# Second attention: score products over all 128 rows, keys in zero-padded tiles, a ring of two head groups

## The chip, the cores and the metric

The kernel runs on one core of one Trainium2 chip. The metric is the device time of one execution in microseconds (us); the kernel before takes 2373.17 us, the median of three runs.

## The reference

A batch of 8 sequences of 512 tokens and 128 features passes six blocks, each added to its input: `ffn0` (32 experts, 8 chosen), `attn0` (causal softmax attention), `ffn0` again, `ffn1` (8 experts, 2 chosen), `attn1` and `ffn1` again. The change lies in `attn1`, the second attention:

```python
qkv = (x @ w_qkv).reshape(Bx, Sx, H, 3 * HD)          # H = 16 heads, HD = 8
scores = jnp.einsum('bhqd,bhkd->bhqk', q, k) / jnp.sqrt(HD)
w = jax.nn.relu(scores)
attn = w / (jnp.sum(w, axis=-1, keepdims=True) + 1e-6)
out = jnp.einsum('bhqk,bhkd->bhqd', attn, v)
y = x + out @ w_out + b_out
return layernorm(y) * gamma + beta                     # and x = x + this
```

So each head has only 8 numbers per token to sum over in a score.

## The kernel before

The six stages run one after another, each over 8 chunks; a chunk (c0 to c7 here) is one sequence of 512 tokens. All data between stages stays in the on-chip memory `x`. In each stage every engine goes through the same list of slots, and the tables `TAIL`, `PREP`, `QKV_AT` and `PUT_AT` say at which slot an engine does a step of the chunk before (its end, "tail") or of the chunk after (its beginning, "prep"). The engines agree through semaphores only; each executes its own list in order.

Precision: a float32 product is made of three fp32r products (high by high, high by low, low by high), called `products` (lines 375 to 377). For the scores the three are put in one contraction instead: each head has 3 x 8 = 24 rows of parts of q and k, padded to 32 rows. q and k go for that through DRAM: ScalarE and VectorE leave the parts in `attn_parts`, SyncE's queue writes them to `parts_dram` (6 transfers, L1314), and reads them back by groups of four heads, 32 rows per head, so that a group fills 128 partitions.

A chunk of `attn1` has 16 slots: 4 groups of four heads by 4 blocks of 128 keys. In slot n (`pe_attn1`, L752 on) TensorE makes four score products (L767), one per head, each 24 rows deep with 128 key columns as weights and 512 queries streaming. Head j lies in partitions 32j to 32j+24 of `k_st` and `q_st`, so that the four use four different row strips of the array. Then come the products with the values of the slot before (`pv1`, L578): for each of four heads 128 rows and 32 output columns, in two instructions, four column strips side by side. ReLU and the move out of PSUM are done by ScalarE (L880, heads 0, 1 and in six slots 3) and VectorE (L1167, the others). There are four score banks, one for each head, so a head's next score product waits until its bank has been emptied.

Around them, in the same slots: the layernorm of the next chunk (VectorE L890 to L907, TensorE turn L489), its q, k and v (TensorE in slots 4, 5 and 7), the last slot's value product and the output projection of the chunk before (slots 0 and 6), the division by the sums (`take_half`, VectorE L1086 to L1098, once in slot 9 and once in the next chunk's slot 1), and the second layernorm (`y_norm` in slot 7, `y_scale` in slot 9, `y_add` on GpSimd in slot 10).

SyncE's list for a chunk of `attn1` (`dma_body`): wait for the parts of the next chunk, write them, then read the four groups of the next chunk, each as one transfer for q (L1328) and one for k (L1333), each as soon as this chunk has made its last score product with that group. `attn0` already keeps its keys in another form, `k_one`: a tile of 128 partitions for every head, with the head's 32 rows in place and zeros elsewhere; its score products (L687, L709) run over all 128 rows.

Of the kernel before, what the change touches and what calls it, by code (L numbers as in the profile page):

```python
# [16 lines left out]
P = 128  # L17
# [40 lines left out]
QUAD = 4  # L58
NQ = H // QUAD
NBLK = S // 32  # L60
ONE = 1
# [94 lines left out]
class AttnMemory:  # L156


    def __init__(self, which, alloc, part):
        def sb(name, shape, dt, stack=part):  # L160
            return alloc(name, shape, dt, stack)

        self.q_st = sb(which + "_q_st", [P, NQ, S], F32R)
        if which == "attn0":
            self.k_one = sb("k_one", [P, NQ, QUAD, S], F32R)
        else:
            self.k_st = sb(which + "_k_st", [P, NQ, S], F32R)
        self.parts = sb(which + "_parts", [P, 2, 2, S], F32R)
        self.v_tok = sb(which + "_v_tok", [P, NT, NQ, QUAD, HD], F32)
        self.v_st = sb(which + "_v_st", [P, NT, NQ, QUAD, PC], F32)  # L170
        self.attn = sb(which + "_attn", [P, NBLK, PC], F32)
        with ExitStack() as shared:
            stack = shared if which == "attn0" else part
            self.o_turn = sb(which + "_o_turn", [P, NBLK, PC], F32, stack)
            self.aT = sb(which + "_aT", [P, S], F32, stack)
        self.aT_hi, self.aT_lo = sb(which + "_aT_hi", [P, S], F32R), sb(which + "_aT_lo", [P, S], F32R)
        if which == "attn0":
            self.rmax = sb("rmax", [P, 2, NT, QUAD], F32)
        else:
            self.xk = sb("attn1_xk", [P, 2, NT, D], F32)  # L180

# [6 lines left out]
def build(nc, x_in, w0, w1, wa, biases, bd3, rows, consts, out, scratch, mixed):  # L188
    nc.disable_value_cache = True
    ctx = ExitStack()  # L190
    with ctx:
# [12 lines left out]
        ident = ident_r[:, :].bitcast(F32)  # L204
        cbf = sb("cbf", [P, NCONST], BF16)
        bd_parts = sb("bd_parts", [96, NPART, D], BF16)
# [238 lines left out]
        def stacks_in(ch):  # L445

            return 32 * (ch.ga + 1) + 48 * (ch.g + 1 if ch.causal else NB)

# [187 lines left out]
        def weight(eng, ch, p):  # L636

            if p == 0:
                eng.wait_ge(wT_ready, ch.gf + 1)

            if p == 1 and ch.first and ch.s:
                eng.wait_ge(o_turned, 2 * ch.stages_before("attn") * NB)
            eng.wait_ge(hid_ready, ROUND + ch.g * NPS + (p - 1 if p > 1 else p - 2))
            eng.matmul(weight_bank(p)[:, :], cbf[0:NPART * E0, C_SEL0 + p * P:C_SEL0 + (p + 1) * P], wT[:, ch.parity, :],
                       start=True, stop=True).then_inc(wb_ready, 1)

        def pe_ffn1(eng, ch, j):
# [15 lines left out]
            if j % HC == 1:  # L663
                e = j // HC
                if e == 0:
                    eng.wait_ge(wT_ready, ch.gf + 1)
                eng.wait_ge(rb_ready, ROUND + ch.g * E1 + e)
                eng.matmul(bank[4][:, :], cbf[0:NPART * E1, C_SEL1 + e * P:C_SEL1 + (e + 1) * P],  # L668
                           wT[0:NPART * E1, ch.parity, :], start=True, stop=True).then_inc(rb_ps, 1)
# [87 lines left out]
        def pe_attn1(eng, ch, n):  # L757

            quad, kb, i = n // NT, n % NT, ch.g * NS1 + n
            if kb == 0:  # L760
                eng.wait_ge(st_in[quad], stacks_in(ch))
            if n == 0 and ch.first:
                eng.wait_ge(ze_ready, ROUND + ch.stages_before("ffn1") * NB * E1)
            for j in HEAD_ORDER:
                rows_ = slice(PC * j, PC * j + NROW * HD)
                eng.wait_ge(p1_ready[j], ROUND + i)
                eng.matmul(bank[j][:, :], mem1.k_st[rows_, quad, kb * P:(kb + 1) * P], mem1.q_st[rows_, quad, :],  # L767
                           start=True, stop=True).then_inc(s1_ps, 1)
            if n:
                pv1(eng, ch, n - 1)  # L770
# [398 lines left out]
        def dve_tail(eng, step, ch):  # L1169
# [20 lines left out]
            if step == "y_norm":  # L1190
# [3 lines left out]
                eng.wait_ge(kept, ch.g + 1)  # L1194
                xk = mem1.xk[:, ch.parity, :, :]
                v = st.mark(eng.tensor_tensor(xk, ob, xk, ALU.add))
# [9 lines left out]
            if step == "y_scale":  # L1206
                xk = mem1.xk[:, ch.parity, :, :]
                eng.wait_ge(y_rstd_ready, ch.g + 1)
# [6 lines left out]
        def pool_prep(eng, step, ch):  # L1215
# [3 lines left out]
            if step == "keep":  # L1219
                eng.wait_ge(ln_steps.sem, ch.G * 13 + 13)  # L1220
                if not ch.first:
                    eng.wait_ge(x_done, ONE + ch.G - 1)
                eng.tensor_tensor(mem1.xk[:, ch.parity, :, :], xn[:, :, :], row_of(1), ALU.add).then_inc(kept, 1)
            if step == "put":
                for quad in range(NQ):
                    put_values(eng, ch, quad)
        def pool_tail(eng, step, ch):
# [3 lines left out]
            if step == "y_add":  # L1231
                eng.wait_ge(tail.sem, 13 * ch.g + 13)
                xk = mem1.xk[:, ch.parity, :, :]
                eng.tensor_tensor(xk, xk, row_of(2), ALU.mult).then_inc(y_scaled, 1)
# [70 lines left out]
        def write_stacks(eng, ch):  # L1305

            if not ch.first or not ch.causal:
                eng.wait_ge(st_in[NQ - 1], stacks_in(ch) - (80 if ch.causal else 32))
            for i in range(2):
# [7 lines left out]
        def read_stacks(eng, ch, g):  # L1317
# [3 lines left out]
            if not ch.first and ch.causal:  # L1321
                eng.wait_ge(st_ready, (ch.g - 1) * NS0 + (g + 1) * NF)
            elif not ch.first:
                eng.wait_ge(s1_ps, ((ch.g - 1) * NS1 + (g + 1) * NT) * QUAD)
            if ch.causal and ch.first and g == 0:
                eng.wait_ge(k_zeroed, H)
            q_src, k_src = (stacks[i, g * QUAD:(g + 1) * QUAD, :, :] for i in range(2))
            eng.dma_start(ch.mem.q_st[:, g, :].bitcast(F32), q_src.rearrange("h r s -> (h r) s")).then_inc(st_in[g], 16)  # L1328
            if ch.causal:
                for j in range(QUAD):  # L1330
                    eng.dma_start(mem0.k_one[PC * j:PC * (j + 1), g, j, :].bitcast(F32), k_src[j]).then_inc(st_in[g], 16)
            else:
                eng.dma_start(mem1.k_st[:, g, :].bitcast(F32), k_src.rearrange("h r s -> (h r) s")).then_inc(st_in[g], 16)  # L1333

# [17 lines left out]
        def dma_body(eng, s, c):  # L1352
# [10 lines left out]
            if ch.kind == "attn0":  # L1363
# [9 lines left out]
                if not ch.last:  # L1373
                    for g in range(2, NQ):
                        read_stacks(eng, after, g)
            elif after is not None and after.kind[:4] == "attn":
                write_stacks(eng, after)
                for g in range(NQ):
                    read_stacks(eng, after, g)
# [45 lines left out]
        def _(eng):  # L1425
# [24 lines left out]
        def _(eng):  # L1450
# [61 lines left out]
        def _(eng):  # L1512
            for counts in (xnT_ps,):
                eng.sem_inc(counts, ONE)
            for counts in (h_used, h1_used, pv1_done):
                eng.sem_inc(counts, ROUND)
            eng.wait_ge(const_ready, 2 + E1 + 1)
            eng.wait_ge(w_lo_done, len(loads))
# [68 lines left out]
```

## Time and profile before

| | |
|---|---|
| time, median of 3 runs | 2373.17 us (2372.46 to 2374.28) |
| the profiled execution | 2367.19 us, of which the span from first to last instruction is 2365.5 us |
| TensorE busy | 2205.1 us, 93% of the span |
| VectorE, ScalarE, GpSimd busy | 1737.0, 1290.2, 922.0 us |
| mean granted TensorE clock | 0.974 of full speed |
| the second attention | 1612 to 1936 us of the span |

The profile is of one execution. A TensorE instruction's duration contains the pipeline behind it, and instructions overlap; the distance from the start of one to the start of the next says what it costs the engine. "Idle before" with a releaser names who ended the wait.

### The profile page before, as it was taken

To read this page: it belongs to the slowest core of one execution; us is meant where nothing else is said; L and a number is where in the kernel's file an instruction comes from. 1 tells how busy PE (TensorE), PEld (TensorE's weight loads), DVE (VectorE), ACT (ScalarE), POOL (GpSimd) and SP (SyncE) were. 2 spreads that over 40 slices of the span, in tenths; PEclk is the share of its full clock that TensorE was granted. 3 is DMA by queue.
4 is the path that set the end of the run, shared out by engine and by line. 5 is a ranking of instruction groups with operands and counts; after the bars stand their busy time and mean duration, and the time that the engine had idled before them with its cause. 6 is when DMAs were issued, how large, how long until landed. Compare 5 with 4: busy or idle time off the path is not lost.

```text
span 2365.5 us, 45578 instructions
## 1 busy us (share of the span) xinstructions
PE 2205.1 (93%) x11232; PEld 1475.3 (62%) x11232; DVE 1737.0 (73%) x3590; ACT 1290.2 (55%) x2000; POOL 922.0 (39%) x903
## 2 busy tenths in 40 slices
PE   2999999999999889999999999999999999999999
PEld 2666666666666666666777777773323236777776
DVE  4676666777777566667568888876767787888886
ACT  3655565455555656565455555555555554555554
POOL 1555455223332445555434444442121224444443
PEclk9999999999999999999999999998979899999999
DMA  3000002233322000000000000012323200000000
GB/s 147 1 0 0 0 0 63 63 86 104 87 80 80 14 13 14 9 9 16 10 1 1 0 0 0 0 37 89 107 71 98 89 10 5 5 4 4 4 4 10
DMA packets 59566, 78.94 MB, mean 33 GB/s; under 512 B 22784, under 2 KB 27104, under 8 KB 59232
## 3 DMA queue, kind: packets, MB, share of 16 engines
q1 hardware_dynamic: 59488, 77.99, 11.0%
q8 instruction: 38, 0.62, 0.1%
q14 instruction: 40, 0.33, 0.0%
HBM read 48.08 MB, written 29.88 MB: 33 GB/s over the span
## 4 chain that ended last, share of the span: by engine, by line
PE 57%; issue 16%; POOL 11%; DVE 11%; ACT 2%; DVEq 1%; DMA 1%; POOLq 1%; SPq 0%; ACTq 0%
PE pair L375 12%; PE pair L377 10%; PE pair L376 10%; POOL h_lo L1293 10%; PE pair L767 3%; PE bank L578 3%; PE pair L578 3%; PE pair L687 2%; PE pair L709 2%; PE bank L564 2%; PE pair L668 2%; PE bank L375 1%; DVE rmax L1123 1%; PE bank L377 1%; PE bank L376 1%
## 5 line engine op out<-in xcount | busy, mean ns | idle before, releaser
L1299 POOL TENSOR_TENSOR h_lo<-hid,h_hi 128x512 fp32r<-128x512 f32 x256 | 330.4, 1291 | 515.7 <-ACT h_hi L851 515.7
L1293 POOL TENSOR_TENSOR h_lo<-hid,h_hi 128x512 fp32r<-128x512 f32 x272 | 351.5, 1293 | 365.2 <-ACT h_hi L817 364.2
L375 PE MATMUL pair<-xnT_hi,w_hi 128*128 (+1 forms) x1056 | 481.7, 456 | 11.0 <-DVE h_lo L1068 8.9
L377 PE MATMUL pair<-xnT_hi,w_lo 128*128 (+1 forms) x1056 | 419.4, 397 | 0.0
L376 PE MATMUL pair<-xnT_lo,w_hi 128*128 (+1 forms) x1056 | 416.5, 394 | 0.0
L375 PE MATMUL pair<-h_hi,w_hi 128*128 128x512 f32 x784 | 327.8, 418 | 14.7 <-POOL h_lo L1293 12.3
L846 ACT ACTIVATE hid<-pair,bias 128x512 f32<-128x512 f32 x256 | 176.3, 689 | 258.9 <-PE pair L377 256.9
L376 PE MATMUL pair<-h_lo,w_hi 128*128 128x512 f32 x784 | 309.6, 395 | 0.0
L377 PE MATMUL pair<-h_hi,w_lo 128*128 128x512 f32 x784 | 309.1, 394 | 0.0
L1066 DVE TENSOR_SCALAR h_hi<-pair,nb 128x512 fp32r<-128x512 f32 x256 | 191.3, 747 | 117.9 <-PE pair L377 116.7
L817 ACT ACTIVATE h_hi<-hid 128x512 fp32r<-128x512 f32 x272 | 171.6, 631 | 179.3 <-DVE hid L1051 164.7
L375 PEld LDWEIGHTS pair<-xnT_hi,w_hi 128*128 128x128 f32 x1056 | 203.1, 192 | 54.6 <-issue 18.6
L821 ACT ACTIVATE gate<-pair,bias 128x512 f32<-128x512 f32 x272 | 185.7, 683 | 89.4 <-PE pair L377 85.8
L869 ACT ACTIVATE probs<-pair 128x1024 f32<-128x1024 f32 x160 | 163.4, 1025 | 129.3 <-PE pair L709 126.1
L1042 DVE SCALAR_TENSOR_TENSOR prod<-pair,bias,gate 128x512 f32<-128x512 f32 x256 | 191.1, 746 | 55.4 <-ACT gate L821 35.6
L880 ACT ACTIVATE probs<-pair 128x512 f32<-128x512 f32 x304 | 163.3, 598 | 120.0 <-PE pair L767 113.3
L377 PEld LDWEIGHTS pair<-xnT_hi,w_lo 128*128 128x128 f32 x1056 | 199.2, 189 | 45.1
L376 PEld LDWEIGHTS pair<-xnT_lo,w_hi 128*128 128x128 f32 x1056 | 200.8, 190 | 34.3
L375 PEld LDWEIGHTS pair<-h_hi,w_hi 128*128 128x128 f32 x784 | 147.5, 188 | 83.2 <-issue 38.5
L1068 DVE SCALAR_TENSOR_TENSOR h_lo<-pair,nb,h_hi 128x512 fp32r<-128x512 f32 x256 | 192.3, 751 | 9.0
L1278 POOL TENSOR_SCALAR_AFFINE_SELECT probs<-probs 128x512 f32<-128x512 f32 (+1 forms) x160 | 87.0, 543 | 264.7 <-ACT probs L869 264.7
L851 ACT ACTIVATE h_hi<-hid 128x512 fp32r<-128x512 f32 x256 | 161.8, 632 | 28.4 <-PE pair L377 3.7
(183 smaller groups left out, 3648.9 us busy)
## 6 DMA issues: line engine op xcount, KB each, us to landing
parts_dram<-attn_parts SPq DMA_DIRECT2D x96, 256.0 KB, 2.9
attn_q_st<-parts_dram SPq DMA_DIRECT2D x64, 256.0 KB, 2.7
k_one<-parts_dram SPq DMA_DIRECT2D x128, 64.0 KB, 2.4
attn_k_st<-parts_dram SPq DMA_DIRECT2D x32, 256.0 KB, 3.0
stage_w<-in_w_dram SPq DMA_DIRECT2D x32, 130.0 KB, 2.1
stage_w<-in_w_dram SPq DMA_DIRECT2D x6, 512.0 KB, 12.4
x<-in_x_dram SPq DMA_DIRECT2D x1, 2048.0 KB, 7.7
mixed_dram<-attn_aT SPq DMA_DIRECT2D x32, 64.0 KB
```

The costliest lines, as they stand in the source:

```text
L375: eng.matmul(o, w_hi_, v_hi, start=start, stop=False, **kw)
L376: eng.matmul(o, w_hi_, v_lo, start=False, stop=False, **kw)
L377: return eng.matmul(o, w_lo_, v_hi, start=False, stop=stop, **kw)
L817: eng.activation(h_hi[:, q % NH0, :], hid[:, q % NHID, :], ACT.Copy).then_inc(hi_ready, 1)
L821: eng.activation(gate[:, p % 2, :], bank[p % 2][:, :], ACT.Silu, bias=bias[:, BG + p:BG + p + 1]).then_inc(silu_ready, 1)
L846: eng.activation(hid[:, i % NHID, :], bank[j % 3][:, :], ACT.Relu, bias=bias[:, B1 + j:B1 + j + 1]).then_inc(hid1_ready, 1)
L869: eng.activation(probs0[:, fill, :, :], pair[ring(("k", n))][:, :, :], ACT.Exp).then_inc(p0_full, 1)
L1042: eng.scalar_tensor_tensor(dst, bank[2 + p % 2][:, :], bias[:, BU + p:BU + p + 1], gate[:, p % 2, :], ALU.add, ALU.mult).then_inc(prod_rea ...
L1066: eng.tensor_scalar(h_hi[:, j % NH1, :], bank[j % 3][:, :], floor, None, ALU.max).then_inc(hi1v_ready, 1)
L1068: eng.scalar_tensor_tensor(h_lo[:, j % NH1, :], bank[j % 3][:, :], floor, h_hi[:, j % NH1, :].bitcast(F32), ALU.max, ALU.subtract).then_in ...
L1293: eng.tensor_tensor(h_lo[:, p % NH0, :], hid[:, p % NHID, :], h_hi[:, p % NH0, :].bitcast(F32), ALU.subtract).then_inc(lo_ready, 1)
L1299: eng.tensor_tensor(h_lo[:, j % NH1, :], hid[:, j // 2 % NHID, :], h_hi[:, j % NH1, :].bitcast(F32), ALU.subtract).then_inc(lo1p_ready, 1)
```

## The change

`attn1` keeps its keys as `attn0` does, in a `k_one` of its own, but for two groups at a time: group g uses place g modulo 2 (`KRING = 2`). A score product takes all 128 rows of `k_one` and of `q_st`; the zeros take the other heads' rows out of the sum. A group of k now comes in four transfers of 32 rows, one for each head. Since the ring holds two groups, groups 2 and 3 of a chunk are read within the chunk, after slots 3 and 7 have made their score products; SyncE does this ahead of the writes for the next chunk and the reads of its groups 0 and 1. The ring's zeros are set once by VectorE after the first chunk of the first `ffn1`. To find room, the residual tile `attn1_xk` and the selector matrices `sel1` take memory of their own, partly that of `sel0`, which is no longer needed then, and the constants come in three copies instead of one.

```diff
@@ class AttnMemory
-            self.k_st = sb(which + "_k_st", [P, NQ, S], F32R)
+            self.k_one = sb("attn1_k_one", [P, KRING, QUAD, S], F32R)
@@ build: memory
-        cbf = sb("cbf", [P, NCONST], BF16)
+        cbf = sb("cbf", [P, C_SEL0], BF16)
+        with ExitStack() as part:
+            sel0 = sb("sel0", [P, NP * P], BF16, part)
+        attn1_xk = sb("attn1_xk", [P, 2, NT, D], F32)
+        sel1 = sb("sel1", [P, E1 * P], BF16)
@@ pe_attn1
             for j in HEAD_ORDER:
-                rows_ = slice(PC * j, PC * j + NROW * HD)
                 eng.wait_ge(p1_ready[j], ROUND + i)
-                eng.matmul(bank[j][:, :], mem1.k_st[rows_, quad, kb * P:(kb + 1) * P], mem1.q_st[rows_, quad, :],
+                eng.matmul(bank[j][:, :], mem1.k_one[:, quad % KRING, j, kb * P:(kb + 1) * P], mem1.q_st[:, quad, :],
                            start=True, stop=True).then_inc(s1_ps, 1)
@@ write_stacks
-                eng.wait_ge(st_in[NQ - 1], stacks_in(ch) - (80 if ch.causal else 32))
+                eng.wait_ge(st_in[NQ - 1], stacks_in(ch) - 80)
@@ read_stacks
-            elif not ch.first:
-                eng.wait_ge(s1_ps, ((ch.g - 1) * NS1 + (g + 1) * NT) * QUAD)
+            elif not ch.first or not ch.causal and g >= KRING:
+                eng.wait_ge(s1_ps, (ch.g * NS1 + (g - KRING + 1) * NT) * QUAD)
...
-                eng.dma_start(mem1.k_st[:, g, :].bitcast(F32), k_src.rearrange("h r s -> (h r) s")).then_inc(st_in[g], 16)
+            for j in range(QUAD):
+                eng.dma_start(ch.mem.k_one[PC * j:PC * (j + 1), g if ch.causal else g % KRING, j, :].bitcast(F32),
+                              k_src[j]).then_inc(st_in[g], 16)
@@ dma_body
-            elif after is not None and after.kind[:4] == "attn":
+            if ch.kind == "attn1":
+                for g in range(KRING, NQ):
+                    read_stacks(eng, ch, g)
+            if ch.kind != "attn0" and after is not None and after.kind[:4] == "attn":
                 write_stacks(eng, after)
-                for g in range(NQ):
+                for g in range(NQ if after.causal else KRING):
                     read_stacks(eng, after, g)
@@ scalar, start of the program
-            eng.activation(cbf[:, :], stage_c[:, 0:NCONST], ACT.Copy).then_inc(const_ready, 1)
+            for dst, a, b in ((cbf, 0, C_SEL0), (sel0, C_SEL0, C_SEL1), (sel1, C_SEL1, NCONST)):
+                eng.activation(dst[:, :], stage_c[:, a:b], ACT.Copy).then_inc(const_ready, 1)
@@ vector, after the first chunk of the first ffn1
                     eng.wait_ge(x_done, ONE + s * NB)
+                    for i in range(KRING):
+                        eng.memset(mem1.k_one[:, i, :, :].bitcast(F32), 0.0).then_inc(k_zeroed, 1)
```

## Rows read from the trace of the kernel before

**Rows 1.** The page: busy time, share and instructions, by engine.
```profile
PE 2205.1 (93%) x11232; PEld 1475.3 (62%) x11232; DVE 1737.0 (73%) x3590; ACT 1290.2 (55%) x2000; POOL 922.0 (39%) x903
```
**Rows 2.** Windows: stage, length, busy by engine, clock, DMA: first and second attention.
```profile
612.00:960.00 348.00, 323.23 (x2001) 225.46 (x2000) 245.17 (x482) 198.03 (x271) 141.16 (x173) 0.99 0.17 45
1612.00:1936.00 324.00, 296.67 (x1786) 105.27 (x1787) 237.07 (x535) 182.52 (x344) 59.99 (x72) 0.86 0.25 80
```
**Rows 3.** The line of the score products (L767): durations, count, first and last start.
```profile
L767 PE MATMUL pair<-attn_q_st,attn_k_st x512: 477/497/792, 1612.9 to 1934.6; 24*128 24x512 f32 x171
```
**Rows 4.** Timeline of TensorE, slots 6 and 7 of c2: start, duration, instruction.
```profile
1707.29 0.51 PE L767 MATMUL pair<-attn_q_st,attn_k_st 24*128 24x512 f32 x4
1707.73 1.07 PE L578 MATMUL pair<-probs,attn_v_st 128*32 128x512 f32 x8
1708.72 0.33 PE L375 MATMUL bank<-wa_hi,xnT_hi 128*128 128x128 f32 x1
...
1710.21 0.50 PE L767 MATMUL pair<-attn_q_st,attn_k_st 24*128 24x512 f32 x4
```
**Rows 5.** Timeline of TensorE, the q product between column strips and row strips.
```profile
1700.86 0.50 PE L375 MATMUL bank<-xnT_hi,wa_hi 128*128 128x512 f32 x1
1701.20 0.39 PE L376 MATMUL bank<-xnT_lo,wa_hi 128*128 128x512 f32 x1
...
1701.76 0.79 PE L767 MATMUL pair<-attn_q_st,attn_k_st 24*128 24x512 f32 x4
```
**Rows 6.** Timeline of TensorE in the first attention, 128-row scores and column strips.
```profile
700.41 0.71 PE L709 MATMUL pair<-attn_q_st,k_one 128*128 128x512 f32 x2
701.06 0.64 PE L564 MATMUL bank<-probs,attn_v_st 128*32 128x256 f32 x8
```
**Rows 7.** Timeline of TensorE, two slots at the lower clock.
```profile
1681.25 0.80 PE L767 MATMUL pair<-attn_q_st,attn_k_st 24*128 24x512 f32 x4
...
1683.84 0.80 PE L767 MATMUL pair<-attn_q_st,attn_k_st 24*128 24x512 f32 x4
```
**Rows 8.** Windows around two falls of the clock; columns as in rows 2.
```profile
1674.80:1678.20 3.40, 0.81 (x7) 0.31 (x3) 3.24 (x5) 0.81 (x2) 2.89 (x3) 1.00 0.01 2
...
1691.80:1695.20 3.40, 2.73 (x19) 1.26 (x16) 3.12 (x11) 2.56 (x5) 1.28 (x2) 1.00 0.30 108
1695.20:1698.60 3.40, 3.40 (x18) 0.49 (x12) 3.13 (x8) 1.50 (x4) 0.00 (x0) 0.51 0.00 0
```
**Rows 9.** Timeline, slots 9 and 10 of c1: VectorE, then TensorE.
```profile
1673.64 0.72 DVE L1086 STREAM_TRANSPOSE attn_o_turn<-pair 128x512 f32<-128x512 f32 x1
...
1675.92 1.50 DVE L1098 TENSOR_TENSOR attn_attn<-attn_o_turn,rden 128x256 f32<-128x256 f32 x1
1677.34 1.27 DVE L1167 TENSOR_SCALAR probs<-pair 128x512 f32<-128x512 f32 x2
...
1673.39 0.50 PE L767 MATMUL pair<-attn_q_st,attn_k_st 24*128 24x512 f32 x4
...
1678.07 1.38 PE L767 MATMUL pair<-attn_q_st,attn_k_st 24*128 24x512 f32 x3 [2.58 <-DVE probs L1167]
```
**Rows 10.** Timeline of VectorE, slot 1 of c1, the other half of the division.
```profile
1654.99 0.43 DVE L1098 TENSOR_TENSOR attn_attn<-attn_o_turn,rden 128x256 f32<-128x256 f32 x1
```
**Rows 11.** Timeline of SyncE's queue, second and first attention; then a time to landing.
```profile
1702.48 4.43 SPq L1314 DMA_DIRECT2D parts_dram<-attn_parts  x6
1709.74 0.33 SPq L1328 DMA_DIRECT2D attn_q_st<-parts_dram  x1
...
674.48 1.82 SPq L1331 DMA_DIRECT2D k_one<-parts_dram  x4
...
k_one<-parts_dram SPq DMA_DIRECT2D x128, 64.0 KB, 2.4
```
**Rows 12.** Timeline in the first `ffn1`: VectorE's zeroing of the values, TensorE behind it.
```profile
1243.05 1.76 DVE L1481 MEMSET attn_v_st<- 128x2048 f32 x1 [0.38 <-issue]
1246.90 0.49 PE L375 MATMUL pair<-xnT_hi,w_hi 128*128 x1 [0.41 <-DVE h_lo L1068]
```

More of the change, by code:

```diff
@@ L59 @@
 NQ = H // QUAD
+KRING = 2
 NBLK = S // 32
@@ L178, in __init__ @@
             self.rmax = sb("rmax", [P, 2, NT, QUAD], F32)
-        else:
-            self.xk = sb("attn1_xk", [P, 2, NT, D], F32)
 def act_heads(n):
@@ L445, in stacks_in @@
         def stacks_in(ch):
-            return 32 * (ch.ga + 1) + 48 * (ch.g + 1 if ch.causal else NB)
+            return 80 * (ch.ga + 1)
         def filled(ch, use):
@@ L643, in weight @@
             eng.wait_ge(hid_ready, ROUND + ch.g * NPS + (p - 1 if p > 1 else p - 2))
-            eng.matmul(weight_bank(p)[:, :], cbf[0:NPART * E0, C_SEL0 + p * P:C_SEL0 + (p + 1) * P], wT[:, ch.parity, :],
+            eng.matmul(weight_bank(p)[:, :], sel0[0:NPART * E0, p * P:(p + 1) * P], wT[:, ch.parity, :],
                        start=True, stop=True).then_inc(wb_ready, 1)
@@ L667, in pe_ffn1 @@
                 eng.wait_ge(rb_ready, ROUND + ch.g * E1 + e)
-                eng.matmul(bank[4][:, :], cbf[0:NPART * E1, C_SEL1 + e * P:C_SEL1 + (e + 1) * P],
+                eng.matmul(bank[4][:, :], sel1[0:NPART * E1, e * P:(e + 1) * P],
                            wT[0:NPART * E1, ch.parity, :], start=True, stop=True).then_inc(rb_ps, 1)
@@ L1194, in dve_tail @@
                 eng.wait_ge(kept, ch.g + 1)
-                xk = mem1.xk[:, ch.parity, :, :]
+                xk = attn1_xk[:, ch.parity, :, :]
                 v = st.mark(eng.tensor_tensor(xk, ob, xk, ALU.add))
@@ L1206, in dve_tail @@
             if step == "y_scale":
-                xk = mem1.xk[:, ch.parity, :, :]
+                xk = attn1_xk[:, ch.parity, :, :]
                 eng.wait_ge(y_rstd_ready, ch.g + 1)
@@ L1222, in pool_prep @@
                     eng.wait_ge(x_done, ONE + ch.G - 1)
-                eng.tensor_tensor(mem1.xk[:, ch.parity, :, :], xn[:, :, :], row_of(1), ALU.add).then_inc(kept, 1)
+                eng.tensor_tensor(attn1_xk[:, ch.parity, :, :], xn[:, :, :], row_of(1), ALU.add).then_inc(kept, 1)
             if step == "put":
@@ L1232, in pool_tail @@
                 eng.wait_ge(tail.sem, 13 * ch.g + 13)
-                xk = mem1.xk[:, ch.parity, :, :]
+                xk = attn1_xk[:, ch.parity, :, :]
                 eng.tensor_tensor(xk, xk, row_of(2), ALU.mult).then_inc(y_scaled, 1)
@@ L1322, in read_stacks @@
                 eng.wait_ge(st_ready, (ch.g - 1) * NS0 + (g + 1) * NF)
-            elif not ch.first:
-                eng.wait_ge(s1_ps, ((ch.g - 1) * NS1 + (g + 1) * NT) * QUAD)
-            if ch.causal and ch.first and g == 0:
-                eng.wait_ge(k_zeroed, H)
+            elif not ch.first or not ch.causal and g >= KRING:
+                eng.wait_ge(s1_ps, (ch.g * NS1 + (g - KRING + 1) * NT) * QUAD)
+            if ch.first and g == 0:
+                eng.wait_ge(k_zeroed, H + (0 if ch.causal else KRING))
             q_src, k_src = (stacks[i, g * QUAD:(g + 1) * QUAD, :, :] for i in range(2))
             eng.dma_start(ch.mem.q_st[:, g, :].bitcast(F32), q_src.rearrange("h r s -> (h r) s")).then_inc(st_in[g], 16)
[L1329 to L1332, printed above, removed]
-                eng.dma_start(mem1.k_st[:, g, :].bitcast(F32), k_src.rearrange("h r s -> (h r) s")).then_inc(st_in[g], 16)
+            for j in range(QUAD):
+                eng.dma_start(ch.mem.k_one[PC * j:PC * (j + 1), g if ch.causal else g % KRING, j, :].bitcast(F32),
+                              k_src[j]).then_inc(st_in[g], 16)
         def heads_out(eng, ch):
@@ L1516, in _ @@
                 eng.sem_inc(counts, ROUND)
-            eng.wait_ge(const_ready, 2 + E1 + 1)
+            eng.wait_ge(const_ready, 4 + E1 + 1)
             eng.wait_ge(w_lo_done, len(loads))
```

## The prediction

> **What bounds the kernel now.** I read the page first. TensorE is busy for 93% of the span [rows 1], so what counts is how long it takes over its own list and what it waits for. The windows by stage come next, since the change touches one stage: the second attention lasts 324 us, with 128 slots (8 chunks of 16), so 2.53 us a slot, and its granted clock is 0.86 where the first attention has 0.99 [rows 2]. The clock has two levels, 1.2 and 2.4 GHz, so 0.86 means that 28% of the stage, 91 us, ran at the lower one. All 512 score products lie in this stage [rows 3].
>
> The timeline gives the cost of a slot where TensorE waits for nothing. At the upper clock the four score products start together and the value products start 0.44 us later (1707.29 to 1707.73); these take 0.99 us (to 1708.72) [rows 4]. A slot is thus 1.43 us. At the lower clock it is 2.59 us (1681.25 to 1683.84) [rows 7]. The q product costs 0.90 us (1700.86 to 1701.76) [rows 5], as does k; v costs 1.49 us (1708.72 to 1710.21) [rows 4], and I take the same for the projection, which has as many instructions, and 0.6 us for the turn of the normed input. That is about 5.4 us for a full chunk and 43 us for eight.
>
> So the 324 us are made up of 128 x 1.43 = 183, plus 43 for the other products, plus 45 for the lower clock (half of the 91 us), and the 53 that are left are waits of TensorE, 6.6 us a chunk. The largest wait is in slot 10. VectorE spends 3.70 us on the division (1673.64 to 1677.34) before it empties the banks of slot 9, and TensorE stands for 2.6 to 2.9 us [rows 9]. In the window with this wait TensorE was busy for 0.81 of 3.40 us. The clock fell at its end. But it fell too at 1695.2 us, where TensorE had been busy for 2.73 of 3.40 us, with row-strip scores of 24 rows and few value products [rows 8]. Slots with half-filled scores keep the clock up badly; this is what the change can win on.
>
> **Score products over 128 rows: dearer.** They no longer start together: one follows the other. The q product shows what fp32r products of 128 rows and 512 columns cost between column strips and strips: 0.34 us from the first to the second, then 0.56 us for the last two, that is 0.23 and 0.33, since the last one before strips is slower again [rows 5]. The first attention has this very sequence, 128-row scores and then column strips: two products take 0.65 us (700.41 to 701.06) [rows 6], the same 0.32 each at the ends. Four are 0.34 + 0.23 + 0.23 + 0.33 = 1.13 us; I take 1.12. Against 0.44 that is 0.68 more a slot, 87 us for 128 slots. From below, four at the inner pitch of 0.23 give 0.92 us, 61 us in all; from above, twice the 0.65 us of two gives 1.30 us, 110 us. I take 87, because the row it rests on has the same neighbours. Slot floor: 1.12 + 0.99 = 2.11 us.
>
> The Trainium skill has a rule against this change: in "TensorE: Matmul & The Clock Gate", Part 3 (Measured speedup), four row strips with 512 columns gain 3.07 times over doing them one by one. By it the scores would go from 0.44 to 1.35 us, 116 us in all (an estimate from that page); the rows say 2.5 times, and the sum goes by the rows.
>
> **The clock: given back, mostly.** In a slot of 2.11 us TensorE now streams over full rows nearly all the time, so the falls with no long wait (1695.2) go; so do second and third stretches at the lower clock after a fall, since even there it works densely. The first attention, with the same forms, has 0.99 [rows 2]. All 45 us would go. But the wait in slot 10 stays: VectorE's 3.70 us stand. VectorE can begin about 0.5 us after slot 9's first score product, ends 3.7 us later, the first freed bank lets TensorE go on 0.73 us after that (1677.34 to 1678.07) [rows 9]: 4.97 us. TensorE gets there after 1.12 + 0.99 + 0.34 = 2.45 us, and waits 2.5 us, then 0.3 us for the other bank. A wait of this length brought the clock down each time before; with dense work before and behind it I let it fall in two chunks of three, for a stretch of about 3.4 us like 1695.2 to 1698.6 [rows 8], costing half less the wait within it: 1.3 us x 5.4 falls = 7 us. From below 0 (never), from above two stretches in each of 8 chunks, 27 us.
>
> **Waits that the longer slot hides.** VectorE empties two banks in 1.27 us [rows 9], well inside a slot of 2.11, and ScalarE has the other half; so ordinary slots no longer wait. In slots 0 to 3 VectorE has the layernorm, the other half of the division and the turn's input to do, and following it by the durations I get 0.9 us of waiting a chunk. With 2.8 in slot 10 that is 3.7 a chunk, 30 us in all for 53 before: 23 us gained. What is late next in the other slots is TensorE itself.
>
> **SyncE's queue.** A group's k is four transfers, 1.82 us of issue for 0.43 before; per chunk 20 reads for 8. The writes for the next chunk used to start at slot 4 or 5 and are now behind the read of group 3, which waits for slot 7's scores, and behind its landing. Chain from there: q 0.34 and k 1.82 issued, 2.4 to land, six writes 4.43, 2.8 until they have landed (1706.91 to 1709.74), the next group 0's issue 2.2 and landing 2.4: 16.4 us [rows 11]. From slot 7's last score product to the next chunk's slot 0 there are about eight slots, 8 x 2.11 plus the wait of 2.8 plus the last value product 0.99, less the product itself, some 20 us or more. It fits, with 4 us to spare. Groups 2 and 3 have four slots, over 8 us, for 4.6. Cost 0; nothing else waits on SyncE in this stage. At the start three copies of constants in place of one add only fixed parts (the columns are the same), ahead of weights that ScalarE then waits for from DMA: 0, at most 0.5.
>
> **Zeros for the ring.** VectorE's zeroing of 2048 columns takes 1.76 us, and already that one leaves TensorE waiting 0.41 us [rows 12]. Two more are 3.5 us ahead of work TensorE needs: nearly all becomes a wait, and such a wait can bring the clock down once more. I take 4 us; 0 at least if there is slack that I don't see, 7 at most (two stretches at the lower clock).
>
> **Sum.** +87 - 45 + 7 - 23 + 4 = +30 us. The profiled execution's own time is 2367.19 us (span 2365.5), which becomes 2397; it is 6 us below the median of the runs, so the forecast on the median is 2373 + 30 = 2403 us. A difference of about 0.2% (5 us) can be told from none.
>
> **Rivals.**
> A, faster: the change of strips costs nothing any more. If a score slot of 128 rows needs neither the extra 0.1 us at its two ends nor the 0.12 us between value products and scores, scores are 4 x 0.22 = 0.87 and a slot 1.74 us: 128 x 0.31 = 40 us more in place of 87, so 2403 - 47 = 2356 us. It decides from a slot floor of about 1.8 us downwards. For it: row strips are gone. Against it: the value products keep their column strips, and the first attention pays at this very seam [rows 6]. The Trainium skill agrees with the rows here ("TensorEngine Tiling (Array Packing)", Key Properties: changing the tiling mode drains TensorE), and by it A is not to be had. 15%.
> B, nearly even: the wait in slot 10 goes. Its division step took 1.50 us there and 0.43 us in slot 1 [rows 9, 10], while GpSimd's `y_add` ran beside it. Were the two to part in the new order, the division is 2 us shorter, the wait 0.8, and the clock doesn't fall: -16 and -7, 2380 us, and with scores between the forecast and their lower bound (1.02 us, -13) 2367. Against it: `y_add` still follows `y_scale` directly. 12%.
> C, slower still: the transfers come late. If the chain of 16.4 us is 7 us longer, through transfers that crowd each other, slot 0 of seven chunks waits 3 us: +21, 2424 us. For it: there are more and smaller transfers, and the writes stand behind two reads. Against it: the DMA share of the stage is 0.25 [rows 2]. 7%.
> That the change doesn't do what it says I exclude; the same tile form runs in the first attention.
>
> **How the numbers follow.** The forecast has 66%, with its own range of 2377 (scores at 0.92 us) to 2423 (falls at their upper bound). A 15%, B 12%, C 7%. For 8 in 10 I go down into A: 2360 to 2426. Faster (under 2368): A and a part of B, 0.18. Within 0.2% (2368 to 2378): the rest of B and the forecast's lower edge, 0.12. Slower: 0.70.
>
> **What would show it.** In the timeline of the new kernel: four score products about 1.1 us before the value products, and 2.1 us from slot to slot (0.9 and 1.75 would be A). In the windows: the stage 350 us long, its clock at 0.95 or more, with falls only behind slot 10. VectorE's division still 3.7 us and TensorE's wait after it 2.5 (B: 1.7 and none). In SyncE's queue: the read of group 0 landed before slot 0 (C: TensorE released by a transfer). In the first `ffn1`: a wait of TensorE of 3 to 4 us behind the zeroing. The prediction is wrong if the slot floor is not near 2.1 us, or if TensorE's waits shrink by much more than 23 us.

## The result: slower by 0.65%, half of what was forecast

| | time, median | |
|---|---|---|
| before | 2372.82 us | 4 runs, 2368.23 to 2374.28 |
| after | 2387.45 us | 4 runs, 2386.36 to 2388.45 |
| ratio after to before | 1.0065 | 95% interval 1.0047 to 1.0082 |

The forecast was 2403 us, with 2360 to 2426 as its range. The change costs 14.6 us on the medians and 21.3 us between the two profiled executions, since that of before (2367.19 us) was quicker than all four of its runs and that of after (2388.45 us) the longest of its four.

The page of the kernel after, its first line, then the windows of the second attention and of the first (columns as in [rows 2]), then the line of the score products:

```profile
PE 2231.0 (93%) x11232; PEld 1518.5 (64%) x11232; DVE 1741.5 (73%) x3592; ACT 1290.1 (54%) x2002; POOL 922.5 (39%) x903
```
```profile
1622.00:1956.00 334.00, 315.41 (x1779) 143.04 (x1781) 237.34 (x534) 182.10 (x344) 60.26 (x72) 0.98 0.26 81
612.00:960.00 348.00, 323.32 (x1987) 225.54 (x1988) 243.28 (x480) 196.17 (x268) 139.48 (x172) 0.98 0.16 45
```
```profile
L769 PE MATMUL pair<-attn_q_st,attn_k_one x512: 387/397/796, 1621.9 to 1955.2; 128*128 128x512 f32 x171
```

The stage is 11.5 us longer (worked out below) in spite of a granted clock of 0.98 for 0.86 [rows 2]. A single score product has become shorter by its record (397 ns for 497 [rows 3]) and all four together much longer; only the distance from start to start says so. The timeline of TensorE in slots 6 to 8 of c2, which answers to [rows 4]:

```profile
1720.93 1.14 PE L769 MATMUL pair<-attn_q_st,attn_k_one 128*128 128x512 f32 x4
1722.00 1.07 PE L581 MATMUL pair<-probs,attn_v_st 128*32 128x512 f32 x8
1723.00 0.33 PE L378 MATMUL bank<-wa_hi,xnT_hi 128*128 128x128 f32 x1
...
1724.39 1.15 PE L769 MATMUL pair<-attn_q_st,attn_k_one 128*128 128x512 f32 x4
1725.47 1.06 PE L581 MATMUL pair<-probs,attn_v_st 128*32 128x512 f32 x8
1726.46 1.19 PE L769 MATMUL pair<-attn_q_st,attn_k_one 128*128 128x512 f32 x4
1727.59 1.06 PE L581 MATMUL pair<-probs,attn_v_st 128*32 128x512 f32 x8
1728.58 1.19 PE L769 MATMUL pair<-attn_q_st,attn_k_one 128*128 128x512 f32 x4
```

From score to score: 1726.46 to 1728.58 is 2.12 us, of which the scores take 1.13 (1726.46 to 1727.59). The forecast had 1.12 and 2.11. After another 128-row product the scores cost only 1.07 to 1.08 us (1720.93 to 1722.00, 1724.39 to 1725.47), and v costs 1.39 us (1723.00 to 1724.39) for 1.49 before: the seam between products of 128 rows and row strips is gone there.

Where the 21.3 us between the profiled executions lie, by comparing when the same TensorE instruction starts in both: 0.5 us at the start of the first attention, 3.4 us between 740 and 860 us of the span, 5.3 us near 1250 us, 11.5 us in the second attention (1612.91 to 1935.07 before, 1621.93 to 1955.55 after), 0.7 us behind it. The 3.4 us are a clock that fell three times there in this execution and not in that of before, in code that the change doesn't touch. The profiled executions of other kernels below have one such fall there (e2), two (e6) or none (e1); how often each kernel has them is not known.

The lengths of the slots, from the starts of their first score product (my table; a star: started at the lower clock):

| slot | 0 | 1 | 2 | 3 | 4 | 5 | 6 | 7 | 8 | 9 | 10 | 11 | 12 | 13 | 14 | 15 | chunk |
|---|---|---|---|---|---|---|---|---|---|---|---|---|---|---|---|---|---|
| before, c1 | 1.18 | 2.61 | 2.69 | 2.46 | 2.53 | 2.92 | 2.92 | 1.43 | 2.17 | 1.59 | 6.26 | 2.59* | 1.91* | 1.82 | 1.51 | 2.88 | 39.5 |
| before, c3 | 1.18 | 2.85 | 3.80* | 3.49* | 2.38 | 2.92 | 2.92 | 1.43 | 2.19 | 1.60 | 6.23 | 2.59* | 2.59* | 2.07* | 1.57 | 2.89 | 42.7 |
| after, c2 | 1.19 | 2.61 | 2.72 | 2.92 | 2.81 | 3.40 | 3.46 | 2.07 | 2.12 | 2.12 | 4.70 | 2.12 | 2.12 | 2.12 | 2.12 | 3.09 | 41.7 |
| after, c3 | 1.18 | 2.61 | 2.70 | 2.92 | 2.81 | 3.40 | 3.46 | 2.07 | 2.12 | 2.12 | 4.93 | 3.43* | 2.13 | 2.12 | 2.12 | 3.08 | 43.2 |

Against the unstarred slots before, slots 3 to 9 have become longer, but for slot 8. Slots 11 to 14 are an even 2.12 us, more than at the upper clock before and less than the starred ones. Slots 0 to 2 have stayed as they were, and slot 10, with the long wait, is over 1 us shorter. The mean of chunks c1 to c6 is 40.96 us before and 42.44 us after.

The wait in slot 10, in the timelines of VectorE and TensorE, answers to [rows 9]:

```profile
1728.92 0.71 DVE L1088 STREAM_TRANSPOSE attn_o_turn<-pair 128x512 f32<-128x512 f32 x1
1729.67 1.05 DVE L1094 TENSOR_SCALAR rden<-attn_o_turn 128x32 f32<-128x32 f32 x1
1731.24 1.50 DVE L1100 TENSOR_TENSOR attn_attn<-attn_o_turn,rden 128x256 f32<-128x256 f32 x1
...
1733.39 1.09 PE L769 MATMUL pair<-attn_q_st,attn_k_one 128*128 128x512 f32 x3 [2.18 <-DVE probs L1169]
```

The zeroing in the first `ffn1`, against [rows 12]: two instructions of 1.76 us, 2.14 us from one to the next, and TensorE waits 4.68 us where it waited 0.41; the granted clock is at the lower level from 1254.6 us on, for 3.4 us.

```profile
1246.96 1.76 DVE L1484 MEMSET attn_k_one<- 128x2048 f32 x1 [0.38 <-issue]
1249.10 1.76 DVE L1484 MEMSET attn_k_one<- 128x2048 f32 x1 [0.38 <-issue]
1251.24 1.76 DVE L1487 MEMSET attn_v_st<- 128x2048 f32 x1 [0.38 <-issue]
...
1255.09 0.79 PE L378 MATMUL pair<-xnT_hi,w_hi 128*128 x1 [4.68 <-DVE h_lo L1070]
```

SyncE's queue, against [rows 11]: the read of group 3 at 1725.57, the writes at 1729.75 and the read of the next chunk's group 0 at 1736.99. Its last issue ends at 1739.2, and with 2.3 us to land it is there at 1741.5; the next chunk's slot 0 starts at 1746.97, 5.5 us later.

```profile
1725.57 0.34 SPq L1330 DMA_DIRECT2D attn_q_st<-parts_dram  x1
1725.95 1.82 SPq L1332 DMA_DIRECT2D attn_k_one<-parts_dram  x4
1729.75 3.81 SPq L1316 DMA_DIRECT2D parts_dram<-attn_parts  x6
1736.99 0.35 SPq L1330 DMA_DIRECT2D attn_q_st<-parts_dram  x1
```

### The profile page after: what moved, and what is told of

It is laid out like the page before. It is cut to its first block, busy times and chain, and to the rows that moved or that the text cites. A ratio compares the mean times of both kernels' runs of the same rounds, so it can differ in the third digit from the quotient of the medians.

```text
span 2386.7 us, 45679 instructions
## 1 busy us (share of the span) xinstructions
PE 2231.0 (93%) x11232; PEld 1518.5 (64%) x11232; DVE 1741.5 (73%) x3592; ACT 1290.1 (54%) x2002; POOL 922.5 (39%) x903
## 4 chain that ended last, share of the span: by engine, by line
PE 58%; issue 16%; POOL 11%; DVE 11%; ACT 1%; DVEq 1%; DMA 1%; POOLq 0%; SPq 0%; ACTq 0%
PE pair L378 12%; PE pair L380 10%; PE pair L379 10%; POOL h_lo L1295 10%; PE pair L769 5%; PE pair L690 2%; PE bank L581 2%; PE bank L567 2%; PE pair L712 2%; PE pair L581 2%; PE pair L671 2%; PE bank L378 1%; DVE rmax L1125 1%; DVE h_hi L1068 1%; PE bank L380 1%
## 5 line engine op out<-in xcount | busy, mean ns | idle before, releaser
L378 PE MATMUL pair<-h_hi,w_hi 128*128 128x512 f32 x784 | 327.6, 418 | 14.6 <-POOL h_lo L1295 12.2
L819 ACT ACTIVATE h_hi<-hid 128x512 fp32r<-128x512 f32 x272 | 171.6, 631 | 179.3 <-DVE hid L1053 164.7
L1169 DVE TENSOR_SCALAR probs<-pair 128x512 f32<-128x512 f32 x208 | 136.1, 685 | 67.6 <-PE pair L769 67.4
## 6 DMA issues: line engine op xcount, KB each, us to landing
stage_w<-in_w_dram SPq DMA_DIRECT2D x6, 512.0 KB, 12.3
```

The lines of the kernel that those rows point to most:

```text
L378: eng.matmul(o, w_hi_, v_hi, start=start, stop=False, **kw)
L819: eng.activation(h_hi[:, q % NH0, :], hid[:, q % NHID, :], ACT.Copy).then_inc(hi_ready, 1)
```

## The experiments

Ratios are to the kernel before in the same session, whose median was 2372.48, 2369.64 and 2369.83 us in the three. "Chunk" is the mean of c1 to c6, "low clock" the time at 1.2 GHz within the stage; both are of the one profiled execution and in us, while the time is the median of the runs.

| kernel | time | ratio, 95% interval | chunk | low clock |
|---|---|---|---|---|
| before | 2372.82 | | 40.96 | 89 |
| after | 2387.45 | 1.0065 (1.0047 to 1.0082) | 42.44 | 10 |
| e1 after, zeros on GpSimd | 2380.22 | 1.0040 (1.0026 to 1.0053) | 42.21 | 10 |
| e2 after, 24-row scores | 2377.45 | 1.0024 (1.0015 to 1.0033) | 40.97 | 89 |
| e3 before, 128-row fillers | 2348.79 | 0.9912 (0.9895 to 0.9929) | 37.19 | 10 |
| e4 after, y_add one slot later | 2387.86 | 1.0074 (1.0061 to 1.0088) | 42.45 | 10 |
| e5 e1 with fillers | 2379.53 | 1.0045 (1.0031 to 1.0059) | 41.74 | 3 |
| e6 after, division alone | 2373.16 | 1.0013 (1.0004 to 1.0022) | 39.74 | 3 |
| e7 e3 with 24-row fillers | 2362.99 | 0.9975 (0.9964 to 0.9985) | 39.66 | 58 |
| e8 before, fillers, division alone | 2336.89 | 0.9866 (0.9851 to 0.9882) | 35.33 | 14 |
| e9 before, division alone | 2348.88 | 0.9913 (0.9900 to 0.9927) | 37.46 | 68 |
| e10 e1, division alone | 2367.52 | 0.9990 (0.9981 to 0.9999) | 39.74 | 3 |
| e11 e8, fillers in slot 11 of c7 | 2334.27 | 0.9852 (0.9836 to 0.9867) | 35.29 | 7 |

**e1. The zeros.** VectorE's zeroing of the ring goes; in its place:

```diff
+                if ch.s == FIRST1 and ch.last and j % 2 == 1 and j // 2 < KRING * QUAD:
+                    ...
+                    eng.memset(mem1.k_one[:, i // QUAD, i % QUAD, :].bitcast(F32), 0.0).then_inc(k_zeroed, 1)
```

> The changed kernel, with the ring's zeros set by GpSimd in eight pieces in the odd slots of the last chunk of the first ffn1, instead of by VectorE after its first chunk. In the changed trace TensorE is 5.3 us later behind that zeroing (3.9 to 9.2 us behind the kernel before), 3.5 us of it the two zeroings and the rest a fall of the clock at 1254.6 us. Theory: this is the zeroing's price and GpSimd is idle in those slots, so about 5 us go: 2382 us, no fall of the clock near 1250 us. Rival: the 5.3 us are luck in when the clock falls, or are only moved to the last chunk: 2387 us as before the edit.

Measured 2380.22 us, 7.2 us less than after, and no fall of the clock near 1250 us. Between 1207 and 1600 us of the span the distance to the kernel before doesn't change (1.6 us throughout, where after went from 3.9 to 9.2). The zeroing's 5.3 us are settled. The two profiled executions are 8.0 us apart, and there 3.4 more are the falls between 740 and 860 us, which this one didn't have; whether they also make up the other 2 us of the medians no run shows.

**e2. The scores alone undone**, with everything else of the change kept:

```diff
+                rows_ = slice(PC * j, PC * j + NROW * HD)
-                eng.matmul(bank[j][:, :], mem1.k_one[:, quad % KRING, j, kb * P:(kb + 1) * P], mem1.q_st[:, quad, :],
+                eng.matmul(bank[j][:, :], mem1.k_one[rows_, quad % KRING, j, kb * P:(kb + 1) * P], mem1.q_st[rows_, quad, :],
```

> The changed kernel with the score products again on 24 rows of each head's strip (taken out of the zero-padded tiles); ring, zeros, 20 transfers a chunk and their order stay. Theory: the whole of the 11.5 us in the stage is the form of the score product. Then a slot without waits is 1.43 us again, the clock of the stage is back at 0.86, the stage takes its 322 us, and the kernel is slower than before by the zeroing alone: 2373 + 5 = 2378 us. Rival: the transfers within the chunk cost something by themselves (TensorE released by a transfer at slot 0, now that slots are shorter): the stage is 3 us or more longer than before, 2381 us or above.

Measured 2377.45 us, chunks of 40.97 us and the clock of before. The window of its stage:

```profile
1619.40:1943.00 323.60, 296.42 (x1783) 104.97 (x1782) 236.75 (x534) 182.44 (x344) 60.00 (x72) 0.86 0.27 83
```

TensorE's busy time and the clock are those of [rows 2] to 0.3 us. From first to last score product the stage takes 322.3 us for 321.7 before. So ring, transfers within the chunk and their order cost no more than the 0.5 us between these two executions (rival C is out), and the form of the score product is the cause both of the longer stage and of the steadier clock.

**e3. The clock without dearer scores.** In the kernel before, products that nobody reads are put where TensorE waits for VectorE: eight ahead of slot 10's scores, two before and two after slot 1's first.

```diff
+            def filler(count):
+                for _ in range(count):
+                    eng.matmul(bank[4][:, :], w1_hi[:, 1, :], w1_hi[:, 1:1 + NT, :], start=True, stop=True)
+            if n in (1, 10):
+                filler(2 if n == 1 else 8)
             for j in HEAD_ORDER:
+                if n == 1 and j == HEAD_ORDER[1]:
+                    filler(2)
```

> The kernel before (row strips, no ring, no zeros) with filler products of 128 rows and 512 columns whose results nobody reads: eight ahead of slot 10's scores and four around the first score product of slot 1, where TensorE waits for VectorE anyway. Theory: what the changed kernel wins in the stage is the clock, and it can be had without dearer scores. The falls behind slots 10 and 1 go, 70 or 75 of the stage's 89 us at the lower clock; half of that less what VectorE then holds up, about 30 us: 2343 us, stage clock 0.97. Rival: VectorE sets the pace, and at the upper clock TensorE only waits longer; the fillers then bring nothing: 2370 to 2376 us with the clock up.

Measured 2348.79 us. The fillers fill the wait of [rows 9], as the timeline of TensorE in slot 9 and 10 of c1 shows, and the stage's clock is 0.98:

```profile
1674.09 1.23 PE L578 MATMUL bank<-probs,attn_v_st 128*32 128x512 f32 x8
1675.25 2.11 PE L766 MATMUL pair<-w_hi 128*128 128x512 f32 x8
1677.29 0.50 PE L775 MATMUL pair<-attn_q_st,attn_k_st 24*128 24x512 f32 x1
1678.36 1.10 PE L775 MATMUL pair<-attn_q_st,attn_k_st 24*128 24x512 f32 x3 [0.57 <-DVE probs L1175]
```
```profile
1616.50:1914.00 297.50, 289.82 (x1870) 116.20 (x1868) 236.18 (x532) 181.85 (x342) 60.33 (x72) 0.98 0.28 87
```

The chunk goes from 40.96 to 37.19 us: the low clock cost 3.8 us a chunk. It is not 30 us for the stage, as c7 still has a fall (10 us at the lower clock from 1902.9 us on) and has become 1.6 us longer; from first to last score product the stage takes 297.7 us for 321.7, 24 us less. That is also less than the 39 us that half of the 79 us of low clock taken away would be: at the upper clock some of that time becomes waits for VectorE. The theory had 2343 us, 6 too low; the fall in c7 is a part of that.

**e4. y_add by slots.** `y_add` from slot 10 to 11, the residual's `keep` from 11 to 12, the bias from 10 to 12, all on GpSimd.

```diff
-(9, "dve", "y_scale"), (10, "pool", "y_add")),
+(9, "dve", "y_scale"), (11, "pool", "y_add")),
...
-    "attn1": (11, 4, 4, 4, 5, 5, 5, 7, 7),
+    "attn1": (12, 4, 4, 4, 5, 5, 5, 7, 7),
...
-            if slot == BIAS_AT:
+            if slot == (BIAS_AT if ch.causal else BIAS_AT + 2):
```

> The changed kernel with GpSimd's y_add one slot later (11), the keep of the residual in slot 12 and the bias in slot 12, so that they run behind VectorE's division of slot 9 and not beside it. Theory: GpSimd beside it makes the division 3.70 us, of which the last step is 1.50 us for 0.43; it becomes 1.7 to 2 us, the wait of TensorE in slot 10 falls from 2.6 to 0.8 us, and the three falls of the clock in the stage go: 8 x 1.8 + 5 = 19 us less, 2368 us. Rival: GpSimd isn't the reason and the division stays 3.7 us: 2387 us; or the later y_add holds up the next chunk: above that.

Measured 2387.86 us: nothing, but it was no test. In its timelines `y_add` (L1236, L1239) still runs beside the division, since no wait holds GpSimd back to the slot in its table:

```profile
1731.03 1.50 DVE L1100 TENSOR_TENSOR attn_attn<-attn_o_turn,rden 128x256 f32<-128x256 f32 x1
...
1729.18 1.28 POOL L1236 TENSOR_TENSOR attn_xk<-attn_xk,row 128x512 f32 x1 [0.22 <-issue]
1730.98 1.26 POOL L1239 TENSOR_TENSOR x<-x,attn_xk  x1 [0.51 <-POOL attn_xk L1236]
```

**e5. The price of the form at an equal clock.** e1 with `filler(8)` ahead of slot 10's scores.

> The changed kernel with the ring's zeros on GpSimd (2380.2 us so far) and eight filler products of 128 rows ahead of slot 10's scores, results unread, as in the kernel before with fillers (2348.8 us). Both now have the clock up nearly everywhere, so this pair shows the price of 128-row scores with the clock taken out. Theory: the two or three falls of the stage go, each 1.5 us: 2376 us, all chunks at 41.7 us. That is 27 us above 2348.8, the price of the form less what longer slots hide of the waits. Rival: in the changed kernel the clock is worth more than these falls, and the fillers bring it below 2370 us.

Measured 2379.53 us, where the theory had 2376. All six chunks are at 41.7 us as expected, so the falls behind slot 10 went; what they gave was small, because e1 had only two of them in c1 to c6 (3 us), and c0 was 0.7 us longer (its fall near 1618 us stayed). The comparison stands: 41.74 against e3's 37.19 is 4.55 us a chunk, the price of 128-row scores with the clock taken out, after what the longer slots hide of the waits. For the stage, from first to last score product, it is 331.4 against 297.7 us: 34 us.

**e6. The division alone.** In the changed kernel:

```diff
             if step == "y_add":
                 eng.wait_ge(tail.sem, 13 * ch.g + 13)
                 xk = attn1_xk[:, ch.parity, :, :]
+                if not ch.last:
+                    eng.wait_ge(attn_ready, 2 * ch.ga + 3)
```

> The changed kernel with one wait more: GpSimd's y_add waits until VectorE's division of slot 9 is done. Moving it by slots left it beside the division, since GpSimd goes through its slots ahead of the others. Theory: alone, the division takes 1.9 us for 3.7, slot 10 goes from 4.7 to 2.9 us and the falls of the clock in the stage go: 8 x 1.8 + 5 = 19 us less, 2368 us, under the kernel before. Rival: the slow steps are VectorE's own (operands in PSUM or in this form), the division stays 3.7 us, and the time 2387 us.

Measured 2373.16 us, 14.3 us less than after on the medians and 12.3 by the ratios (1.0065 and 1.0013), since the two ran in different sessions. Division and `y_add` one after the other:

```profile
1724.26 0.71 DVE L1088 STREAM_TRANSPOSE attn_o_turn<-pair 128x512 f32<-128x512 f32 x1
1725.01 0.19 DVE L1094 TENSOR_SCALAR rden<-attn_o_turn 128x32 f32<-128x32 f32 x1
1725.71 0.43 DVE L1100 TENSOR_TENSOR attn_attn<-attn_o_turn,rden 128x256 f32<-128x256 f32 x1
...
1726.52 1.28 POOL L1238 TENSOR_TENSOR attn_xk<-attn_xk,row 128x512 f32 x1 [5.09 <-DVE attn_attn L1100]
```

The division takes 1.8 us for 3.7, slot 10 2.77 us for 4.7, and of the falls one is left, in c7. Chunks: 39.74 us, 2.0 less than after's without a fall. The 19 us forecast were too many, as the division gives its gain in six chunks only: c0 has no `y_add` of a chunk before it, and c7, which prepares an `ffn1`, has a slot 11 of 5.96 us for 3.68, 3.8 us over the floor of 2.12.

**e7. Rows or busy time.** e3's fillers with 24 rows in place of 128:

```diff
-                    eng.matmul(bank[4][:, :], w1_hi[:, 1, :], w1_hi[:, 1:1 + NT, :], start=True, stop=True)
+                    eng.matmul(bank[4][:, :], w1_hi[0:NROW * HD, 1, :], w1_hi[0:NROW * HD, 1:1 + NT, :], start=True, stop=True)
```

> The kernel before with the fillers of the run that gave 2348.8 us, but 24 rows deep instead of 128: the same places, count, columns and streaming time, so TensorE's busy time is the same. Theory: what keeps the clock up is how much of the array works, which is why slots of 24-row scores and short waits lose it; then these fillers do little, the clock falls behind slot 10 and in slot 1 as in the kernel before, and the time is 2368 to 2376 us. Rival: busy time is what counts, the rows don't matter: 2349 us, clock up. It also tells whether the changed kernel's steady clock comes from the 128 rows or only from the longer busy time of its scores.

Measured 2362.99 us, between the two: 58 us at the lower clock for e3's 10. In c2, TensorE is busy for 4.01 of the 4.40 us that end behind the fillers (first row), and the clock falls all the same (second row):

```profile
1714.00:1718.40 4.40, 4.01 (x25) 2.08 (x21) 4.20 (x7) 1.46 (x4) 3.12 (x3) 1.00 0.19 73
1718.40:1728.60 10.20, 9.81 (x43) 2.32 (x47) 4.79 (x8) 4.14 (x9) 2.62 (x4) 0.50 0.15 51
```

The two edits differ only in the rows of these products, and e3 has no fall in c0 to c6 where this kernel has one in every chunk but c1. The busy time is not quite the same, though: at this place e3's TensorE is busy for 4.23 of 4.40 us. That busy time alone doesn't decide is shown better by the kernel after: in the 4.40 us from 1729.0 on, in c2's wait, its TensorE is busy for 2.22 us, and the clock holds; over the stage it is busy for 94% (315.41 of 334 us) with a clock of 0.98, this kernel for 97% (302.93 of 312.5) with one of 0.91. Nor does a single stretch decide: the same one a chunk earlier (1676.8 to 1681.2), also 4.01 of 4.40 us, kept the clock. The forecast for this run, 2368 to 2376, was too high: 24 rows hold it in part (c1, 37.20 us, kept the clock).

**e8. Both, on row strips.** e3 with e6's wait, three fillers for eight in slot 10.

```diff
-                filler(2 if n == 1 else 8)
+                filler(2 if n == 1 else 3)
...
                 xk = mem1.xk[:, ch.parity, :, :]
+                if not ch.last:
+                    eng.wait_ge(attn_ready, 2 * ch.ga + 3)
```

> The kernel before (row strips) with 128-row fillers, three in slot 10 and four in slot 1, and with GpSimd's y_add waiting for the division of slot 9. If the wait in slot 10 is VectorE's division slowed by GpSimd, both gains add: 2348.8 less 7 or 8 x 1.3 us = 2339 us, chunks of 36 us. Rival: the shorter division is taken back by y_add coming later (the residual of the next chunk stands behind it on GpSimd) or fewer fillers let the clock fall again: 2348 us or more.

Measured 2336.89 us, chunks of 35.33 us, 12 us under e3 on the medians and 11 by the ratios. The forecast was 2339 us with chunks of 36.

**e9. The division alone, on row strips.** The kernel before with e6's wait.

> The kernel before with GpSimd's y_add waiting for the division of slot 9, and no fillers. In the changed kernel this took 14 us (2387.5 to 2373.2), 8 in the changed kernel's seven chunks from the division and the rest from falls of the clock that went. Theory: with row strips the shorter wait saves its 1.8 us a chunk, 13 us, and the clock still falls in many chunks, since the 24-row slots stay what they are: 2355 to 2360 us, stage clock under 0.93. Rival: the wait in slot 10 was the only cause of the falls; then the clock is up, and the time is that of the run with fillers and this wait, 2337 us.

Measured 2348.88 us: less than the theory's 2355 to 2360 and more than the rival's 2337. The clock still falls (68 us of the stage, for 89 before), so 24-row slots lose it also with a wait of under a microsecond in slot 10. But low clock cost less than I had reckoned. Slots 11 to 14 of c1, with a fall of 6.9 us, take 8.84 us for e8's 6.73: 2.1 us and not 3.4, since e8 waits in some of them. Three quarters of the low clock stayed (68 of 89 us), and yet two thirds of e8's gain were there (2369.83 - 2348.88 = 21 us of e8's 33, 2369.64 - 2336.89).

**e10. The change with its side costs mended**: e1 and e6 together.

> The changed kernel with both of its side costs mended: zeros by GpSimd, and y_add waiting for the division; no fillers. Theory: the savings add, 2387.5 less 7 less 14: 2366 us, under the kernel before by 4 to 6 us, and 29 us above the row strips with fillers and the same wait (2336.9), which is the price of 128-row scores at an equal clock. Rival: one saving takes from the other (both take away falls of the clock): 2370 us or more.

Measured 2367.52 us. The savings add to 20 us on the medians (18 by the ratios), and the changed kernel is then 2.3 us under the kernel before (ratio 0.9990, 0.9981 to 0.9999): the interval only just leaves out none, and 2.3 us is under the 5 us that the prediction had set for telling. Against row strips with the same wait and fillers (e8) it is 31 us slower (29 by the ratios).

**e11. The last chunk.** e8 with twelve more fillers in slot 11 of c7.

```diff
+            if n == 11 and ch.last:
+                filler(12)
```

> The row strips with fillers and the waiting y_add (2336.9 us), and twelve more fillers in slot 11 of the last chunk alone, where TensorE stands 2.7 us for VectorE's routing of the next ffn1 and the clock then falls (1891.0 us, twice). Theory: that fall goes, 6.8 us at the lower clock, 3 us: 2334 us. Rival: the slots behind it are held by VectorE anyway: 2337 us.

Measured 2334.27 us, 2.6 us under e8; the fall at 1891 us is gone. The intervals of the two overlap, so only e11's distance to the kernel before is settled: 1.5% faster.

## Why the prediction was right, and where its size was off

The direction, the mechanism and the range held; the time was 15.6 us too high, and the stage, forecast at 350 us, takes 334. Step by step, for the stage by the two profiled executions:

- **Scores, +87.** Right. 1.13 us a slot in the open and 2.12 us from slot to slot; 128 x 0.69 = 88, by slots without a wait; it is a term of the sum, not what the change cost. Rival A (1.74 us a slot, 2356 us) is out: the seam to the column strips of the value products stays.
- **The clock, -45 and +7.** Right as it was reckoned, at half the time at the lower clock: -38 against -39 (89 us before, 10 after). What this price is worth is another matter. e3 took the same 79 us away and its stage became 24 us shorter, so some 15 us of the term are time in which TensorE, at the upper clock, would have waited for VectorE. The sum of clock and waits isn't touched by this, but how it divides between the two is. e2 shows that it was the form of the scores; e7, with the busy times of the kernel after, that the rows of a product count. The falls that stayed are where they were expected, behind slot 10, in three chunks rather than five.
- **Seams, not in the sum.** In the rows for the q product I saw 0.33 us ahead of the strips and used them only to price the new scores. That q, k, v and the projection would lose this seam was missed: q and k 0.80 and 0.69 us (slots 3 and 4 of c2, less 2.12) for 0.90, v 1.39 for 1.49, some 0.1 to 0.2 us at each, about 5 us for the stage.
- **Waits, -23.** This is the term that was mis-sized. I took 53 us before as what was left of 324 after 43 us of other products, but eight full chunks of them are too many: c0 has no projection, c7 no q, k and v. With 38 us the waits before were 58. After, a chunk like c2 is 41.68 - 16 x 2.12 - 4.4 (q, k, projection, v, turn) = 3.3 us of waits, 27 for eight, where I had 30. So they fell by some 31, not 23; the prediction had called much more than 23 a sign of being wrong, and 8 more is on the way there. Together with the seams this is nearly all of the 14.5 us between the stage's +26 by my terms and the 11.5 measured.
- **Zeros, +4.** 5.3 us in the trace, shown by e1; I had left out 0.38 us of issue with each and taken only 0.5 us for everything beyond the 3.5 of the two instructions, the fall of the clock with it.
- **SyncE, 0.** Right: 5.5 us to spare for the 4 forecast, and e2's stage is as long as before. Rival C is out.
- **Rival B**, the division beside `y_add`: the mechanism is real (e6), but the change doesn't part the two, as argued.
- **Outside these terms.** Elsewhere the profiled execution lost 4.6 us that no term had, 3.4 of them the falls between 740 and 860 us; this made the miss smaller. By profiled executions it is 8.6 us (2397 for 2388.45). The other 7 are luck in which execution was profiled: the one before was 6 us below its median, so I put the new median 6 us above its profiled execution too, and it is 1.0 below. So the 15.6 us are 8 of waits, 5 of seams and 1.5 left over in the stage, less 1.3 of zeros and 4.6 elsewhere, plus 7 from the choice of execution.

The rule of the Trainium skill weighed in the prediction ("TensorE: Matmul & The Clock Gate", Part 3, Measured speedup: four row strips gain 3.07 times) was the less exact here: four products cost 1.13 us for 0.44, 2.6 times.

## What to carry to other kernels

Here, padding a shallow contraction with zeros to full rows bought a steadier TensorE clock and gave up products that run side by side. The clock was worth 3.8 us a chunk (e3) and the side by side 4.55 (e5 against e3), so the trade loses. First ask whether the clock can be held more cheaply: full-row products without a use, in waits that are there anyway, brought it back in seven of eight chunks (2348.8 us), at the price of 1.6 us in the last, and taking away the wait's cause added to it (2336.9).

When a wait is put down to an engine, look at what runs beside that engine while it is slow. Two VectorE instructions that take 1.05 and 1.50 us in one slot and 0.19 and 0.43 us in another are the finding; a wait added on GpSimd was worth 12 to 14 us in the changed kernel and 21 us in the kernel before.

## What the runs showed of the hardware

Two of VectorE's small operations on SBUF took longer while GpSimd's ran. In the kernel after, the 0.19 us step started at 1729.67 and lasted until 1730.72, while GpSimd's L1236 ran from 1729.40 to 1730.68; alone (e6) it took 0.19. The division's last step, 0.43 us alone, took 1.50 from 1731.24 on, beside GpSimd's L1239 from 1731.19 to 1732.45. The Trainium skill has this in "SBUF — State Buffer", Who interferes with whom: a VectorE instruction with two SBUF inputs contends with a GpSimd instruction that reads SBUF, one in a two-port mode with any, and whoever comes second is blocked for the whole instruction. The trace agrees for the last step, which has two SBUF inputs: 1.50 us for 0.43. The other has one SBUF input, and no run shows whether it was in a two-port mode.

The granted clock fell behind 4.4 us in which TensorE was busy for 4.01 us, most of it with 24-row products (e7, c2), and stayed up with 128-row fillers in their place (e3, 4.23 of 4.40 us). In the kernel after it stayed up through 4.4 us with only 2.22 us of work, of 128 rows. Busy time alone does not tell whether the clock will hold.
